# A conv-LSTM and mixture-of-experts block on one core: the second tile's 1/deviation rows spread by TensorE instead of through memory

## The reference, cut to what matters

```
n  = (x - mean_c(x)) / sqrt(var_c(x) + 1e-6)       # over the 64 channels of each pixel
fs = conv(n, w_itos, taps "row above" and "this row") + b_itos
for row j in 0..31:                                # a recurrence down the rows
    pre = conv(h, w_stos, 3 taps across columns) + b_stos + fs[row j]
    i, g, f, o = split(pre)
    h_new = c * sigmoid(o);  c = sigmoid(f)*c + sigmoid(i)*tanh(g);  h = h_new
x  = x + hs
t  = tokens(x);  t = t + FFN(layernorm(t))         # 32 experts, each takes its 8 best tokens of an image
```

## Time and profile before

| | |
|---|---|
| profiled execution, its own time | 204.0 us |
| its span, first to last instruction | 202.2 us |
| runs (median) | 205.27, 203.98, 205.28 us (205.27) |
| TensorE matmul busy | 178.2 us, 88% |
| VectorE busy | 165.6 us, 82% |
| GpSimd busy | 125.9 us, 62% |
| ScalarE busy | 109.8 us, 54% |
| mean granted TensorE clock | 0.983 |
| GpSimd waiting for the broadcasts into rb | 6.1 us in 2 waits, longest 4.5 us |
| TensorE (matmul) waiting, 12 to 42 us: GpSimd r (404) / GpSimd x_split (395) / VectorE fc (718) | 1.2 / 1.1 / 0.2 us |

### The profile page before, as it was taken

The page is one execution under the profiler, slowest core; times in us unless marked ns, Lnnn a source line. Parts: engine busy times, 40 slices in busy tenths (PEclk is TensorE's granted clock), DMA queues, the critical chain, the costliest instruction groups (busy, mean ns, idle before and its releaser), DMA issues.

```text
span 202.2 us, 10852 instructions
## 1 busy us (share of the span) xinstructions
PE 178.2 (88%) x4675; PEld 146.5 (72%) x4675; DVE 165.6 (82%) x605; ACT 109.8 (54%) x265; POOL 125.9 (62%) x114
## 2 busy tenths in 40 slices
PE   0899995999989999999999999999988988998800
PEld 1688884988869987987988889788755767684200
DVE  0898797899999899899989978978989999246960
ACT  2554543775645566664666666666468796540000
POOL 4456259698997988989798799399168740000000
PEclk9999999999999999999999999999999999999985
DMA  5754332412423412333231351521550231000896
GB/s 122 169 116 112 79 85 57 109 55 78 89 76 89 110 53 61 99 66 107 63 107 44 82 140 38 138 59 53 144 122 0 80 98 38 6 3 24 239 356 216
DMA packets 29120, 19.12 MB, mean 95 GB/s; under 512 B 2464, under 2 KB 28048, under 8 KB 29072
## 3 DMA queue, kind: packets, MB, share of 16 engines
q1 hardware_dynamic: 27440, 15.87, 30.5%
q10 hardware_dynamic: 1632, 2.56, 4.1%
HBM read 14.12 MB, written 4.30 MB: 91 GB/s over the span
## 4 chain that ended last, share of the span: by engine, by line
PE 61%; DVE 21%; issue 6%; POOL 4%; DMA 2%; ACT 1%; SPq 0%; DVEq 0%; POOLq 0%
PE ps L947 40%; PE ps L938 10%; PE ps L1007 4%; DMA xc<-in_x 2%; DVE ps L715 2%; DVE tail_room L931 2%; DVE xtok L931 2%; DVE st L674 2%; DVE lg L872 2%; DVE x_split L867 2%; POOL r L404 2%; PE ps L1072 1%; DVE v L662 1%; POOL xc L382 1%; DVE cands L861 1%
## 5 line engine op out<-in xcount | busy, mean ns | idle before, releaser
L947 PE MATMUL ps<-x_split,w_hi 64*64 64x256 f16 x1000 | 49.9, 273 | 2.6 <-DVE fc L718 1.3
L947 PEld LDWEIGHTS ps<-x_split,w_hi 64*64 64x64 f16 x1000 | 25.1, 106 | 14.9 <-issue 8.1
L382 POOL TENSOR_TENSOR xc<-xc,h 128x256 f32<-128x256 f32 x31 | 22.7, 733 | 20.5 <-DVE h_lo L699 20.5
L715 DVE TENSOR_TENSOR ps<-sg_i,ps 64x256 f32<-64x256 f32 x62 | 26.7, 430 | 6.8 <-ACT ps L513 5.1
L947 PE MATMUL ps<-h_hi,w_hi 64*64 64x256 f16 x750 | 31.8, 271 | 0.0
L947 PE MATMUL ps<-h_lo,w_hi 64*64 64x256 f16 x750 | 31.8, 271 | 0.0
L947 PE MATMUL ps<-h_hi,w_lo 64*64 64x256 f16 x750 | 31.8, 271 | 0.0
L499 ACT ACTIVATE ps<-ps,bias 128x256 f32<-128x256 f32 x32 | 14.3, 447 | 30.1 <-PE ps L947 30.1
L947 PE MATMUL ps<-x_split,w_lo 64*64 64x256 f16 x500 | 24.5, 269 | 0.0
L938 PE MATMUL ps<-ident,xc 128*128 128x128 f32 x128 | 18.5, 288 | 6.7 <-DMA xc<-in_x 5.2
L674 DVE BATCH_NORM_STATS2 st<-ps 128x6 f32<-128x64 f32 x128 | 18.6, 217 | 5.7 <-PE ps L938 5.7
(11 more groups left out here) (130 smaller groups left out, 331.0 us busy)
## 6 DMA issues: line engine op xcount, KB each, us to landing
xc<-in_x SPq DMA_DIRECT2D x14, 256.0 KB, 3.7
rb_xr<-scratch SPq DMA_DIRECT2D x14, 256.0 KB, 4.3
w1s<-in_L_ffn_weight SPq DMA_DIRECT2D x8, 256.0 KB, 3.5
w2s<-in_L_ffn_weight SPq DMA_DIRECT2D x8, 256.0 KB, 3.6
rbf<-scratch SPq DMA_DIRECT2D x24, 64.0 KB, 2.3
out<-xtok SPq DMA_DIRECT2D x4, 256.0 KB, 5.2
out<-xtok ACTq DMA_DIRECT2D x4, 256.0 KB, 5.8
out<-tail_room SPq DMA_DIRECT2D x3, 256.0 KB, 4.4
```

The costliest lines, as they stand in the source:

```text
L382: p.tensor_tensor(here, here, h32[:, i % 2, :].rearrange("p (b w) -> p b w", w=W), ALU.add) \
L715: v.tensor_tensor(ps_ig[half(h), :], sg_i[half(1 - h), :], pre[G][half(1 - h), 0:COLS], ALU.mult) \
L947: ins = pe.matmul(pre[gate][to, 0:COLS], w[half(h), tap, C * GATE_ORDER[gate]:][:, 0:C], data[half(h)], start=first and m == 0, stop=s_don ...
```

## The change

Tile 1 no longer goes through memory. In its place TensorE multiplies: with a column of r0 (128 pixels x 1, read 64 times over) as the stationary operand and 64 columns of the identity as the moving one, the product puts that column, as a row of 64 pixels, on 64 partitions. Sixteen such products (8 pairs x 2 halves) fill the 128 x 512 PSUM bank `ps_lg` with two of the four rows; ScalarE copies the bank into `rb`; the other two rows follow in a second round. The first round stands where turn_r0(1) stood (`inside`, step 1), the second in `between` of step 1; the copies are in ScalarE's steps 1 (after the hi part) and 2 (before it). GpSimd does both halves of scale_rows(1) before rsqrt0(2). Tiles 2 to 7 go through memory as before, with semaphore counts one lower.

```diff
-                q.wait_ge(s_r0_kept, u)
+                q.wait_ge(s_r0_kept, u - 1)
...
-            spread_r0(1)
...
             def scale_rows(u, k):
-                p.wait_ge(s_rb_in, 2 * DMA * u)
+                if u == 1:
+                    p.wait_ge(s_rb_kept, k + 1)
+                else:
+                    p.wait_ge(s_rb_in, 2 * DMA * (u - 1))
...
                 if t == 0:
                     residual(0, 1)
                     scale_rows(1, 0)
+                    scale_rows(1, 1)
                     rsqrt0(2)
+                    lo_of_x(1, 0)
                     residual(0, 2)
-                    lo_of_x(1, 0)
-                    scale_rows(1, 1)
...
                 a.activation(sg_i[:, :], pre[I][:, 0:COLS], ACT.Sigmoid, bias=bias[:, 0:1]).then_inc(s_sg_i, 1)
-                if n == 1:
-                    keep_r0t(1)
+                if n == 2:
+                    keep_rb(1)
                 a.wait_ge(s_h32, n + 1)
                 hi_part(par, 1 - par)
+                if n == 1:
+                    keep_rb(0)
...
+            def keep_rb(k):
+                a.wait_ge(s_r0_spread, k + 1)
+                a.activation(rb[:, :, 2 * W * k:2 * W * k + 2 * W], ps_lg.rearrange("p (b t) -> p b t", b=NB), ACT.Copy) \
+                    .then_inc(s_rb_kept, 1)
...
+            def spread_r0_here(k):
+
+                pe.wait_ge(s_r0, 3)
+                wait(pe, s_rb_kept, k)
+                for b in range(NB):
+                    for h in range(2):
+                        ins = pe.matmul(ps_lg[half(h), 2 * W * b:2 * W * b + 2 * W],
+                                        r0[:, 1, 2 * b + h:2 * b + h + 1].to_broadcast([128, C]),
+                                        ident[:, 2 * W * k:2 * W * k + 2 * W], start=True, stop=True)
+                ins.then_inc(s_r0_spread, 1)
...
                 if i == 1 and t == 0:
                     pe.wait_ge(s_x_stats, 4)
-                    turn_r0(1)
+                    spread_r0_here(0)
...
+                if i == 1 and t == 0:
+                    spread_r0_here(1)
                 if i == 3 and t == 0:
-                    pe.wait_ge(s_r0_kept, 1)
+                    pe.wait_ge(s_rb_kept, 2)
```

More of the change, by code:

```diff
@@ L203, in metaformer @@
         s_r0 = sem("s_r0")
+        s_r0_spread = sem("s_r0_spread")
+        s_rb_kept = sem("s_rb_kept")
         s_r0_turned = sem("s_r0_turned")
@@ L296, in spread_r0 @@
             def spread_r0(u):
-                q.wait_ge(s_r0_kept, u)
+                q.wait_ge(s_r0_kept, u - 1)
                 q.dma_start(scratch0[u % 2], r0t[:, u % 2, :]).then_inc(s_r0_stored, DMA)
-                q.wait_ge(s_r0_stored, DMA * u)
+                q.wait_ge(s_r0_stored, DMA * (u - 1))
                 wait(q, s_xr, 2 * (u - 1))
@@ L402, in rsqrt0 @@
                 if u > 2:
-                    p.wait_ge(s_r0_turned, u - 2)
+                    p.wait_ge(s_r0_spread, 2)
+                    wait(p, s_r0_turned, u - 3)
                 p.tensor_tensor(r0[:, u % 2, :], v0[:, 3, :], pow_exp[:, :], ALU.pow).then_inc(s_r0, 1)
@@ L521, in keep_tokens @@
                         .then_inc(s_xtok, 1)
+            def keep_rb(k):
+                a.wait_ge(s_r0_spread, k + 1)
+                a.activation(rb[:, :, 2 * W * k:2 * W * k + 2 * W], ps_lg.rearrange("p (b t) -> p b t", b=NB), ACT.Copy) \
+                    .then_inc(s_rb_kept, 1)
             def keep_r0t(u):
-                a.wait_ge(s_r0_turned, u)
-                wait(a, s_r0_stored, DMA * (u - 2))
+                a.wait_ge(s_r0_turned, u - 1)
+                wait(a, s_r0_stored, DMA * (u - 3))
                 a.activation(r0t[:, u % 2, :], ps_r[0:B, 0:TOK], ACT.Copy).then_inc(s_r0_kept, 1)
@@ L781, in keep_gate @@
                 v.wait_ge(s_gate_turned, 1)
-                v.wait_ge(s_r0_kept, 2)
+                v.wait_ge(s_r0_kept, 1)
                 v.tensor_copy(gw[:, :], ps_lg[:, 256:256 + 2 * E]).then_inc(s_gate_kept, 1)
@@ L1021, in inside @@
                     if t + 1 < NT:
-                        pe.wait_ge(s_r0_kept, t + 1)
+                        pe.wait_ge(s_r0_kept, t)
                     else:
```

## The result

The change made the kernel slower: 206.78 us median of 7 runs (205.99 to 207.28) against 204.69 us (203.87 to 205.28); ratio 1.0093, 95% interval 1.0065 to 1.0121, some 1.9 us. The forecast was 204.9 us, 0.4 us faster than before, with a range of 203.2 to 206.7; the time lies 0.08 us above that range, and the change made the kernel slower where I had it a little faster. That the miss of the range is so small is luck: the three runs from which I took 205.27 us as the time before had a median 0.6 us above that of the seven. The profiled execution after is the median one, 206.78 us, span 205.0; the one before was near its lowest.

What follows compares the result with a forecast made beforehand. Taken as bound: tile 0's wait chain through GpSimd, VectorE from 41.2 to 57 us, then TensorE to 150. Tile 0's 0.2 us loss and tile 1 came to -0.4: 205.27 - 0.4 = 204.9 us, range 203.2 to 206.7.

Steps and rivals of the forecast that it cites:

- (1): Products on TensorE: 1.0 us per round, ends 0.96 and 2.1; with the transpose gone, 1.8 us more work.
- (2): TensorE alone in tile 0: could recover 2.34 us of waits, pays 1.8, so about 0.5 us early.
- Rival D: Product rounds bound by weight loads: S = 1.5 us gives +1.2, S = 2.1 gives +2.4, 207.7 us; chance 0.11.
- (3): ScalarE in tile 0: two copies at 0.60 us; the second, 26.33 to 26.93, delays step 2's hi part to about 27.3.
- (4): GpSimd in tile 0: scale_rows(1, 1) from 26.96 to 28.24; TensorE's 0.99 and 1.11 us waits go.
- (5): VectorE's lo part of step 2 held by scale_rows(1, 1), i*g 1.9 us late; TensorE's 0.5 us gain becomes 0.2 loss.
- Rival C: The lo part of step 2 is not held; TensorE keeps -0.5 to -0.7, 204.7 us; chance 0.11.
- Rival E: GpSimd's power instruction holds the lo part of step 2 to 31.15: 2.9 us more, 208.4; chance 0.03.
- (6): Tile 2's memory trip: r0t copy 1.9 us later, broadcasts issued and scale_rows(2, 0) started 0.67 us or more later.
- (7): Tile 1: VectorE's variances and step 6 lo part meet GpSimd's residual and scale_rows(2, 1): +0.35 or -0.4 us; -0.4 taken.
- Case B: Tile 1: step 6's lo part slips in at GpSimd's handover, ends near 45.9, 0.6 better less 0.2: -0.4 us; chance 0.38.
- a shift at 57 us reaches the end whole: After 57.05 TensorE runs almost without a gap to 150 us, so any shift by 57 us carries to the end.

Runs made afterwards that it cites:

- hi_first: Changed kernel, but in step 2 ScalarE makes the hi part before copying the second round into rb; ratio to the kernel before 1.0061.
- pool_order: Changed kernel with GpSimd's order in tile 0 as before, scale_rows(1, 1) last; ratio to the kernel before 1.0073.
- fill: Changed kernel with GpSimd's power instruction for tile 3's r0 moved ahead of scale_rows(2, 0); ratio to the kernel before 0.9999.
- products_fill: Kernel before plus 32 unread products in step 1, and tile 3's r0 power instruction ahead of scale_rows(2, 0); ratio to the kernel before 1.0007.
- late_rows_fill: Kernel before with tile 2's broadcasts held back, and tile 3's r0 power instruction ahead of scale_rows(2, 0); ratio to the kernel before 1.0046.
- products_alone: Kernel before plus the change's 32 products in step 1, result unread, way through memory kept; ratio to the kernel before 1.0096.
- early_load: Changed kernel with tile 4's two loads of x issued after the new h of steps 1 and 2, not 2 and 3; ratio to the kernel before 1.0040.
- late_rows: Kernel before with SP holding tile 2's broadcasts until VectorE's lo part of step 4 is done; ratio to the kernel before 1.0143.
- trip_first: Changed kernel with tile 2's store and broadcasts ahead of the second load of tile 4 on SP's queue; ratio to the kernel before 1.0073.

## Why the prediction was wrong

- (1), (2) The products: 1.08 us a round (20.50 to 21.58), forecast 1.0. Right in form and nearly in size. Rival D falls: weight loads hide.
- (3), (4) Copies of 0.58 and 0.60 us, TensorE's waits of 0.99 and 1.11 us gone. Right, with scale_rows(1, 1) at 27.74 (net 27.3, forecast 26.96) a little late.
- (5) The lo part of step 2 held: right at the end of tile 0, and shown by hi_first and pool_order. Rival C falls. Rival E falls too, since in pool_order the lo part ran at 0.43 us inside a power instruction. The sum, +0.2 at rows_of_x(4, (F, G)), measured +0.45 net; 2 x 0.08 of these 0.25 us are the products. But pool_order shows that this loss does not reach T3 by itself, so it was not a term of the end.
- (6) The r0t copy was 2.15 us later (net), forecast 1.9. The store's gap was 2.64 us, beyond the largest of the trace (2.41), where I took 1.4 to 2.4. Together that put scale_rows(2, 0) net 2.3 us late, where I had 0.7 to 1.7. In the kernel before this gap is 2.60 us and also ends with scale_rows(1, 1); I read it as that wait and never asked what the store alone took. It was the row nearest to the case, with the same load ahead of it.
- (7) **This step failed.** I followed GpSimd's lateness to VectorE's hold in step 6 and then gave all that comes after one price, 0.2 us "in the token scalings near 53". There the runs show 1.2: the lo part of step 8 starts net 1.23 us later than before, though VectorE came to step 8 only 0.09 us late, because GpSimd's queue goes on without a gap from the late rows to the end of the token scalings (net 56.6 instead of 55.2) and holds three variances instead of two. The same queue makes TensorE wait 1.23 us for the power instruction of r1. Before, that instruction ended at 51.37 and the transpose began at 51.51; 0.15 us pass between the two after the change as well, where TensorE waits (53.24 to 53.39), so there was hardly any slack.
- What shows it: `fill`, `products_fill` and `late_rows_fill` change only GpSimd's queue and take away all, nearly all and two thirds of the loss; so this queue is the cause. That it reaches the end through the held variances and not through the wait for r1 is read from the profiles (T3 above). No run moved the variances alone.
- Case B in step 6 came out in size (the lo part ended at 46.15, net 45.7, forecast 45.9), but not for its reason. It was to slip in between residual and scale_rows. With the rows 2.3 us late GpSimd was in its power instruction (43.73 to 46.64) all through the variances and the lo part of step 6, and that held nothing: 0.17 and 0.43 us. That is luck.
- The claim that a shift at 57 us reaches the end whole: nearly. From T3 to T5 another 0.43 us is lost, where near 90 us two of VectorE's variances were held for 0.85 and 1.08 us instead of 0.41 and 1.08. That this belongs to the change and is not chance is only argued: from T3 to T5 hi_first and products_alone lose a similar 0.54 and 0.51 us, early_load 0.03, late_rows nothing. What follows T5 differs from run to run. The sign that I had named for a wrong prediction, that TensorE would not wait for `fc` of step 3, did not come; it does wait for it (0.30 us at 35.74).

## What to carry to other kernels

Take a late arrival to the end of the queue it arrives at, not to the first engine that it meets: add up all that stands behind it in order, and compare with when each result is wanted, and also with what another engine does at that time, since a held instruction is a wait that no semaphore shows. A wait with ready work behind it in the same queue is the cheap thing to mend; here moving one instruction ahead of the wait undid 1.9 us. And when a change takes away the wait that covered a transfer, the transfer's own time has to be found, from a row in the same company of other transfers.

## What the runs showed of the hardware

An 8 KB store was followed by its broadcasts after 1.35 us with no load issued just ahead of it (early_load, trip_first; 1.35 to 1.62 in seven such runs) and after 2.64 us when the last load of x had been issued 0.7 us ahead of it (2.27 to 2.86 in eight). The broadcasts took 5.0 us to GpSimd's start after the change and 6.3 with a load right behind them (trip_first).

Several VectorE instructions in a row can each be held by successive GpSimd ones. In step 8 after the change (the lines are in the section on the result) three variances took 1.19, 1.07 and 0.96 us while GpSimd made a lo part and scaled tokens twice; unheld, they take 0.16 to 0.18 us. Each held one lasted about as long as one GpSimd instruction, so this burst cost 3.2 us instead of 0.5. In the kernel before the same place had two held ones (1.08 and 1.07 us) and one of 0.17. I had priced such a meeting as one wait.
